# Multiplying the attention exponentials by their reciprocal row sums on GpSimd instead of VectorE, in the local layers of a six-stage decoder

## The reference, cut to what matters

```python
def local_attention(q, k, v):          # 16 heads of width 64, window 32
    ...
    sim = jnp.einsum('bhwie,bhwje->bhwij', bq, bk2) * QK_SCALE
    sim = jnp.where(mask, -jnp.finfo(sim.dtype).max, sim)
    attn = jax.nn.softmax(sim, -1)
    out = jnp.einsum('bhwij,bhwje->bhwie', attn, bv2)
...
for i in range(DEPTH):                 # DEPTH = 6
    x = attn_layer(shift_tokens(x), Wqkv[i], q_scale[i], k_scale[i], Wo[i]) + x
    x = ffn_layer(shift_tokens(x), ln_g[i], ln_b[i], W1[i], b1[i], W2[i], b2[i]) + x
```

## Time and profile before

| | us |
|---|---|
| median of the runs | 4233.79 |
| runs | 4235.33, 4232.25 |
| profiled execution, first to last instruction (span) | 4234.2 |
| first to last multiply L938 (96 sequences, 192 halves) | 767.3 to 3372.0 |

### The profile page before, as it was taken

The page is one execution under the profiler, slowest core; times in us unless marked ns, Lnnn a source line. Parts: engine busy times, 40 slices in busy tenths (PEclk is TensorE's granted clock), DMA queues, the critical chain, the costliest instruction groups (busy, mean ns, idle before and its releaser), DMA issues.

```text
span 4234.2 us, 59682 instructions
## 1 busy us (share of the span) xinstructions
PE 3541.2 (84%) x21595; PEld 2601.5 (61%) x21707; DVE 2524.6 (60%) x4741; ACT 2216.8 (52%) x6207; POOL 709.7 (17%) x612
## 2 busy tenths in 40 slices
PE   5888888788888888888888888888888788888998
PEld 3666655566666666666666666666666655655666
DVE  2444434677777777777777777777777634444222
ACT  2433332566666665666666666666666535453332
POOL 0000000222222222222222222221222100000000
PEclk7666666999999999999999999999999967666999
DMA  5000000000000000000000000000000000000000
GB/s 140 0 0 0 0 0 0 1 0 0 0 26 0 0 0 27 0 0 0 26 0 0 0 26 0 0 0 1 1 0 0 0 0 0 0 0 0 3 2 5
DMA packets 36830, 27.61 MB, mean 7 GB/s; under 512 B 15092, under 2 KB 32526, under 8 KB 35982
## 3 DMA queue, kind: packets, MB, share of 16 engines
q1 hardware_dynamic: 36750, 26.57, 2.1%
HBM read 25.52 MB, written 1.05 MB: 6 GB/s over the span
## 4 chain that ended last, share of the span: by engine, by line
PE 70%; DVE 16%; ACT 8%; issue 3%; POOL 2%; SPq 1%; DVEq 0%; POOLq 0%; DMA 0%; ACTq 0%
PE P L461 8%; PE P L518 7%; PE P L503 5%; PE P L525 5%; PE P L343 5%; PE P L543 4%; PE P L325 3%; PE P L672 3%; PE P L657 3%; DVE bufA L899 3%; DVE bufC L901 3%; DVE bufC L942 3%; PE P L320 3%; PE P L321 2%; PE P L384 2%
## 5 line engine op out<-in xcount | busy, mean ns | idle before, releaser
L1172 POOL TENSOR_TENSOR rnorm<-sumsq_g,const_mhalf 128x16 f32<-128x16 f32 x192 | 554.5, 2905 | 1704.0 <-DVE sumsq_g L887 1704.0
L1292 ACT ACTIVATE bufA<-P,bias,rnorm 128x128 f32<-128x128 f32 x1536 | 679.0, 465 | 139.6 <-DVE bias L929 139.5
L1220 ACT ACTIVATE bufB<-P 128x512 f32<-128x512 f32 (+3 forms) x528 | 344.0, 651 | 579.5 <-PE P L483 316.0
L461 PE MATMUL P<-f_wqkv,xcT 128*128 128x512 f32 x1152 | 539.5, 604 | 73.5 <-DVE xcT L879 71.5
L518 PE MATMUL P<-bufC,vals 128*64 128x128 f32 x3072 | 312.8, 284 | 201.9 <-DVE bufC L942 201.9
L518 PEld LDWEIGHTS P<-bufC,vals 128*64 128x64 f32 x3072 | 265.2, 140 | 236.4 <-DVE bufC L942 224.9
L1220 ACT ACTIVATE vals<-P 128x1024 f32<-128x1024 f32 (+2 forms) x144 | 113.6, 789 | 542.0 <-PE P L321 332.6
L461 PEld LDWEIGHTS P<-f_wqkv,xcT 128*128 128x128 f32 x1152 | 205.1, 191 | 278.3 <-issue 259.7
L482 PE MATMUL P<-ident,bufA 128*128 128x128 f32 x1536 | 346.5, 273 | 4.1 <-DVE bufC L901 3.0
L483 PE MATMUL P<-ident,bufC 128*128 128x128 f32 x1536 | 345.8, 273 | 0.0
L1147 POOL TENSOR_TENSOR veps<-mv,const_eps 128x1 f32<-128x1 f32 x208 | 39.9, 192 | 1800.6 <-DVE mv L699 1800.6
(11 more groups left out here) (220 smaller groups left out, 6618.7 us busy)
## 6 DMA issues: line engine op xcount, KB each, us to landing
f_wqkv<-in_L_ffn_Wqkv SPq DMA_DIRECT2D x6, 1536.0 KB
f_wo<-in_L_ffn_Wo SPq DMA_DIRECT2D x6, 512.0 KB
m_w<-in_L_ffn_ew SPq DMA_DIRECT2D x1, 2048.0 KB
m_w<-in_L_ffn_ew SPq DMA_DIRECT2D x8, 256.0 KB
f_w<-in_L_ffn_W SPq DMA_DIRECT2D x6, 341.0 KB
out_x<-x_all SPq DMA_DIRECT2D x4, 256.0 KB, 2.3
f_w<-in_L_ffn_W SPq DMA_DIRECT2D x12, 64.0 KB
m_w<-in_L_ffn_sh_w SPq DMA_DIRECT2D x2, 256.0 KB
```

The costliest lines, as they stand in the source:

```text
L461: ins = pe.matmul(P[:, j, at + k * 512:at + (k + 1) * 512], xcT[:, j, 0:D], f_wqkv[:, p, lo:lo + 512], start=True, stop=True)
L1172: pool.tensor_tensor(rnorm[:, j, hs], sumsq_g[:, j, hs], const_mhalf[:], ALU.pow).then_inc(f["rn_" + s], 1)
L1220: return act.activation(dst, src, ACT.Copy, scale=scale)
L1292: ins = act.activation(bufA[:, j, k * 128:(k + 1) * 128], P[:, j, k * 128:(k + 1) * 128], ACT.Exp, bias=bias[:, j, k:k + 1], scale=rnorm[: ...
```

## The change

The reciprocal of the row sums stays on VectorE. The multiply of the exponentials by it leaves VectorE's list and becomes a step `probs_scaled` of GpSimd, one for each half, of the same shape and still in place in bufA. VectorE's own wait for the reciprocal goes with it; GpSimd waits for the reciprocal instead and gives the same semaphore f["pn"] on to TensorE. In GpSimd's list of a period the two steps stand first, ahead of k_norms, q_norms and inv_std_local. The lists of the other engines and the buffers stay as they are.

```diff
--- before.py
+++ after.py
@@ -933,9 +933,6 @@
                 hs = slice(8 * u, 8 * u + 8)
                 dve.wait_ge(core["probs"], part(CORE_B + n + 1, u))
                 dve.reciprocal(rz[:, j, hs], zsum[:, j, hs]).then_inc(core["rz"], 1)
-                dve.wait_ge(core["rz"], av_cnt(n, u))
-                e = slots(bufA[:, j, u * 1024:(u + 1) * 1024], 8, 128)
-                dve.tensor_tensor(e, e, cols(rz[:, j, hs], 128), ALU.mult).then_inc(f["pn"], 1)
 
             def keep_turned(j, p, q, n, u):
                 dve.wait_ge(core["probsT"], part(CORE_B + n + 1, u))
@@ -1180,8 +1177,13 @@
             def inv_std_local(j, p, q, n):
                 inv_std(norm_back, BATCH + n + 1, j)
 
+            def probs_scaled(j, p, q, n, u):
+                pool.wait_ge(core["rz"], av_cnt(n, u))
+                e = slots(bufA[:, j, u * 1024:(u + 1) * 1024], 8, 128)
+                pool.tensor_tensor(e, e, cols(rz[:, j, 8 * u:8 * u + 8], 128), ALU.mult).then_inc(f["pn"], 1)
+
             def period(b, f):
-                in_turn((k_norms, f), (q_norms, f), (inv_std_local, b))
+                in_turn((probs_scaled, b, 0), (probs_scaled, b, 1), (k_norms, f), (q_norms, f), (inv_std_local, b))
 
             over_layers(pool, period)
```

## The result

The changed kernel took 4321.55 us (median of 4320.17 and 4322.93) against 4233.79: a ratio of 1.0199, 95% interval 1.0183 to 1.0216. It is 88 us slower, where 103 were forecast (4337, range 4290 to 4425). The interval holds 1.02, so the runs don't decide whether the change costs more or less than 2%; the forecast had put 0.72 on more. Executions of one kernel differ by a few us, which is why the medians lie 88 apart.

A forecast was written before the change was run, and what follows sets the result against it. No single engine fills the local layers; the order of waits between engines bounds the 27.21 us period. Half 1's result 1.07 us late, times 96 periods, adds 103 us to 4234.2: 4337, range 4290 to 4425.

The forecast's parts named there:

- The place and the mechanism: Local layers, half 1's multiply on GpSimd: its late result delays TensorE's transposes, 1.07 us in each of 96 periods.
- the chain: One 27.21 us period's waits between engines, read back from what ended last; it wants half 1's multiply result at 1509.87.
- half 0 stayed covered: Half 0's transposes reach VectorE at 1506.76, wanted at 1507.10: 0.34 us to spare, no cost up to a 2.69 us multiply.
- the slip: TensorE's transposes of half 1 start 1.07 us late; v_proj, out_proj b0, weigh b1 and the next period move equally.
- VectorE's row to the power's: Bounds for GpSimd's multiply: 1.225 us for it on VectorE, 2.905 us for GpSimd's power of 16 elements.
- the prediction's own formula: Half 1's slip: reciprocal's end 1508.40, GpSimd start 0.08, multiply, 0.05 to TensorE, against 1509.87, plus 0.06 from rest: 1.07 us.
- rival 5: TensorE's clock falls after the added rest, doubling transposes b1 and v_proj: 2.74 us more a period, 263 more, 4600; chance 0.05.
- PEclk under 0.98 in the local layers: Sign in the changed profile that TensorE's clock falls, which would make the forecast wrong; it was 1.00 before.
- rival 1: GpSimd's multiply takes 2.905 us, so both halves come late: 177 us, 4411; chance 0.08.
- rival 2: GpSimd and VectorE exclude each other; rotate_q waits for the first multiply, 0.91 us a period, 87 us more, 4424; chance 0.07.
- rival 3: TensorE's 0.68 us wait ahead of out_proj b1 absorbs part, leaving 0.39 us a period: 37 us, 4271; chance 0.06.
- rival 4: GpSimd multiplies as fast as VectorE, 1.225 us, so half 1 is ready at 1509.76 and nothing moves: 4234; chance 0.04.

## Why the prediction was right, and where it was off

*The place and the mechanism were right.* Half 1 was 0.2 us off the chain before, and the GpSimd multiply put it on the chain; half 0 stayed covered; VectorE's two multiplies bought nothing, because rotate_q waits for ScalarE's square; the slip went through TensorE's list to the end of the period undiminished. The runs with one half each show the first two, the profile after the others.

*The multiply was mis-sized.* I took 2.35 us, two thirds of the way from VectorE's row to the power's; it measured 1.897, within the bounds and nearer to the lower row than my choice. With it the prediction's own formula gives 1508.40 + 0.08 + 1.90 + 0.05 - 1509.87 + 0.06 = 0.62 us, against 0.64 measured; 61 us instead of 103. The estimates of 2.25 and 2.40 us, worked out from the figures of the Trainium skill (GPSIMD Engine Reference, Performance versus the Vector engine), are too high for this instruction; its word that such work belongs on VectorE holds, since 1.90 stands against 1.23.

*The clock was sized as all or nothing.* The forecast's sum held nothing for it, and rival 5, with a chance of 0.05, held 263 us on top of the 103: a fall in every period. It came in part, about 17 us, in more than one period of four. I blamed the new rest of 1.0 us for it, and that is wrong: filling that rest changed nothing. The falls went when v_proj was moved into the old rest ahead of weigh b0, and with that rest in place they come more often as the period grows. The two misses have opposite signs, 42 us too much and some 17 too little, with 6 outside the local layers too little as well (103 - 42 + 17 + 6 = 84, the difference of the spans). That the total came out nearer than its terms is luck. By its terms alone, without the clock, the prediction with the right length of the multiply would have said 4295. The sign "PEclk under 0.98 in the local layers" was too coarse to show this: the mean is 0.98, and only the distances of the periods tell.

*The other rivals.* Both halves late (rival 1) fell with the multiply's length. That the two engines get in each other's way (rival 2) happens, but not with rotate_q; it took a VectorE multiply with two inputs in SBUF to meet it. Nothing was absorbed (rival 3): 8.80 us from the transposes to x_shifted against 8.73. "Not slower" (rival 4) would have needed 1.34 us.

## What to carry to other kernels

Relieving an engine that is busy three quarters of the time buys nothing where its next instruction waits for another engine; look up that next instruction's releaser before moving work away. In a chain of waits the distance of the moved result to its user is the whole margin: here 0.2 us, against a product that lasts 0.67 us longer. And look for a rest that an independent step already in the list can fill: moving v_proj two places forward in TensorE's order gave 1.3%, and with it the question where the multiply runs lost its weight.

## What the runs showed of the hardware

- GpSimd's product of 128x1024 float32 with a broadcast operand, in place, takes 1.897 us, 1.55 times VectorE's 1.225; 128x512 takes 1.040.
- Beside a two-input VectorE multiply of 0.69 us, the 128x512 one takes 1.544.
- With a rest of 2.0 us on TensorE in each period, 8 to 30 of 95 periods are long, most of them by a fall of the granted clock to 1.2 GHz (0.50 in the change at 1481 to 1482 us), and more of them as the period grows from 27.21 to 27.85 us; with v_proj moved into that rest, a longest rest of about 1 us and a period of 27.86, only the three long periods common to all traces are left. A long period with such a fall is mostly 1.2 to 1.6 us longer than a regular one.
